# Clamping in VectorE's second pass, scaling of the weighed values on ScalarE or VectorE, and their addition to x on GpSimd

## The reference

```
x = x + 0.5 * ffn(layernorm(x)); x = x + attn(layernorm(x)); x = x + 0.5 * ffn(layernorm(x))

# attn, per head h and batch b, i >= j (causal)
s    = Re(qr_i . conj(kr_j))                       # q, k complex, 64 wide, rotated by position
E    = exp(clip(-mu * |i - j|, -30, 0))
V    = sigma_sq / (2 mu) * (1 - E*E) + eta_sq + gamma_sq
maha = maximum(qn_i + E*E * kn_j - 2 * E * s, 0) / V
logits = coef * log1p(maha / nu) - 0.5 * DH * log(V)
out  = softmax(logits) @ v;   y = [Re out, Im out] @ Wo
```

## Time and profile before

| | |
|---|---|
| median of 3 runs | 1684.14 us |
| profiled execution, its own time | 1685.38 us |
| its span, first to last instruction | 1683.6 us |
| matrix engine (PE), matmuls | 1624.1 us, 96% |
| VectorE (DVE) | 1494.5 us, 89% |
| ScalarE (ACT) | 1443.1 us, 86% |
| GpSimd (POOL) | 1013.6 us, 60% |

### The profile page before, as it was taken

The page is one execution under the profiler, slowest core; times in us unless marked ns, Lnnn a source line. Parts: engine busy times, 40 slices in busy tenths (PEclk is TensorE's granted clock), DMA queues, the critical chain, the costliest instruction groups (busy, mean ns, idle before and its releaser), DMA issues. The chain is left out here.

```text
span 1683.6 us, 31247 instructions
## 1 busy us (share of the span) xinstructions
PE 1624.1 (96%) x9690; PEld 1227.8 (73%) x9690; DVE 1494.5 (89%) x3380; ACT 1443.1 (86%) x2909; POOL 1013.6 (60%) x954
## 2 busy tenths in 40 slices
PE   5999988999999999999999999999999999899998
PEld 4787865777776777677777777777776776677876
DVE  6878878999999999999999999999999989977665
ACT  6677678999999999999999999999999998765765
POOL 3564556666666666665766666666666656245555
PEclk9999999999999999999999999999999999999999
DMA  6000022232223323232222323232232322100000
GB/s 178 1 1 1 1 97 73 64 92 64 76 70 76 79 64 85 58 82 70 75 74 64 92 64 76 55 92 69 74 84 60 80 59 51 26 8 7 13 13 13
DMA packets 50484, 100.05 MB, mean 59 GB/s; under 512 B 8208, under 2 KB 25872, under 8 KB 50320
## 3 DMA queue, kind: packets, MB, share of 16 engines
q1 hardware_dynamic: 50320, 98.07, 22.7%
HBM read 17.95 MB, written 5.24 MB: 14 GB/s over the span
## 5 line engine op out<-in xcount | busy, mean ns | idle before, releaser
L1500 POOL TENSOR_TENSOR early<-early 128x1024 f32<-128x1024 f32 x127 | 303.7, 2391 | 421.4 <-PE pS L1191 227.6
L661 POOL TENSOR_TENSOR hid_lo_d<-hid_d,hid_hi_d 128x512 fp32r<-128x512 f32 x176 | 231.4, 1315 | 218.4 <-ACT hid_hi_d L566 211.8
L1392 ACT ACTIVATE early<-early,qnorm 128x128 f32<-128x128 f32 (+3 forms) x512 | 246.6, 552 | 68.0 <-DVE early L1591 67.3
L1191 PE MATMUL pS<-early 128*128 128x128 f32 (+3 forms) x1024 | 297.6, 433 | 0.4 <-PEq L115 0.4
L1376 ACT ACTIVATE early<-early,nmax 128x128 f32<-128x128 f32 (+3 forms) x512 | 280.9, 558 | 7.7 <-DVE nmax L1578 7.4
L1191 PEld LDWEIGHTS pS<-early 128*128 128x128 f32 x1024 | 164.7, 191 | 96.1 <-issue 61.4
L1587 DVE SCALAR_TENSOR_TENSOR pS<-pS,ek 128x1280 f32<-128x1280 f32 x128 | 190.9, 1492 | 43.5 <-PE pS L1191 41.9
L1509 POOL TENSOR_TENSOR ek<-early 128x128 f32<-128x128 f32 (+3 forms) x256 | 216.1, 877 | 3.0 <-ACT early L1384 2.6
L1509 POOL TENSOR_TENSOR ek<-decay,early 128x128 f32<-128x128 f32 (+3 forms) x256 | 215.0, 873 | 0.0
L1233 PE MATMUL pS<-ident,early 128*128 128x128 f32 x1280 | 184.9, 278 | 13.3 <-DVE early L1591 7.0
L1405 ACT ACTIVATE early<-early,params 128x512 f32<-128x512 f32 (+1 forms) x256 | 196.4, 816 | 0.0
(11 more groups left out here) (393 smaller groups left out, 3752.5 us busy)
## 6 DMA issues: line engine op xcount, KB each, us to landing
early<-early SPq DMA_DIRECT2D x263, 256.0 KB, 3.4
early<-trig_d SPq DMA_DIRECT2D x64, 64.0 KB, 2.0
trig_d<-early SPq DMA_DIRECT2D x3, 1024.0 KB, 6.9
early<-in_w SPq DMA_DIRECT2D x3, 704.0 KB, 8.7
x_sb<-in_x SPq DMA_DIRECT2D x4, 512.0 KB, 8.3
early<-in_wqk SPq DMA_DIRECT2D x16, 128.0 KB, 3.4
cos<-trig_d SPq DMA_DIRECT2D x32, 64.0 KB, 2.2
sin<-trig_d SPq DMA_DIRECT2D x32, 64.0 KB, 2.0
```

The lines of the kernel that those rows point to most:

```text
L661: g.tensor_tensor(hid_lo[:, par], hid[:, par], hid_hi[:, par].bitcast(F32), ALU.subtract).then_inc(lo_done, 1)
L1191: last = pe.matmul(s.pS[:, span(I)], rot[:, I * P:(I + 1) * P], rot[:, N:N + (I + 1) * P], start=True, stop=True)
L1392: last = a.activation(u[:, span(I)], u[:, span(I)], ACT.Relu, bias=qnorm[:, r % 2, I:I + 1])
L1500: g.tensor_tensor(rot[:], by_cos[:], crossed[:], ALU.add).then_inc(S["rot_done"], 1)
```

## The change

- The clamp moves. GpSimd makes three columns for each pair from the query norms where it made one: `base` = query norm + U_MIN, `floor` = max(base * 2^-21, U_MIN), `low` = floor - base. The second pass on VectorE becomes four custom instructions (one per row tile) u = max(min(pS + ek, HIGHEST), low), and ScalarE's logarithm takes `base` as its bias, in four instructions where there were two. `clamp` is gone.
- The order of the product changes: the first pass multiplies, pS = -2 s * E, and the second adds ek, which is now E * E * kn. So ek is made from `decay2` and waits for it; it waits for the pair's second pass (t_done), where it waited for the first (w_done), because ek is now read there. `decay2` has two more buffers for even heads.
- `accumulate` is split. Scaling p7 by rinv into a new buffer `weighed` (512 columns, one buffer) is ScalarE's in steps of odd heads (four instructions, two ahead of soften and two behind key_norms) and VectorE's in the others (one instruction, ahead of `distances`). Adding `weighed` to x is GpSimd's, at the end of its step. The scaling waits for acc_done of the pair before; `weigh` waits for y_done (scaling) in place of acc_done.
- To make room in SBUF, the low half of W2 goes to DRAM at the start and comes back in step 123, both by a DMA from GpSimd.

The diff's core; the first `normalise_out` is ScalarE's, `accumulate` GpSimd's, the second `normalise_out` VectorE's.

```diff
             def distances(i, r):
-                wait(v, S["s_done"], n + 1)
-                wait(v, S["ek_done"], n + 1)
-                v.scalar_tensor_tensor(s.pS[:, 0:SW], s.pS[:, 0:SW], -2.0, ek[:], ALU.mult, ALU.add).then_inc(S["w_done"], 1)
-                wait(v, S["w_done"], n + 1)
+                v.wait_ge(S["decay_done"], i * 2 + r // B + 1)
+                wait(v, expanded[par], 48 * (i + 1) if par else 64 * i)
+                v.wait_ge(S["s_done"], n + 1)
+                v.scalar_tensor_tensor(s.pS[:, 0:SW], s.pS[:, 0:SW], -2.0, decay[par][:, 0:SW],
+                                       ALU.mult, ALU.mult).then_inc(S["w_done"], 1)
+                v.wait_ge(S["w_done"], n + 1)
+                v.wait_ge(S["ek_done"], n + 1)
+                v.wait_ge(S["qn_done"], n + 1)
                 wait(v, S["zred_done"], 2 * n)
-                for half, _ in HALVES:
-                    v.tensor_tensor(u[:, half], s.pS[:, half], decay[par][:, half], ALU.mult).then_inc(S["t_done"], 1)
+                for _, pieces in HALVES:
+                    for I in pieces:
+                        last = v._custom_dve(bass.dve_ops.TENSOR_ADD_SAT, out=u[:, span(I)], in0=s.pS[:, span(I)],
+                                             in1=ek[:, span(I)], s0=HIGHEST, s1=low[:, r % 2, I:I + 1])
+                    last.then_inc(S["t_done"], 1)
...
+            def on_scalar(i, r):
+
+                return (r + 3) % STEPS >= B and live(i, r + 3)
...
+            def normalise_out(i, r, tiles):
...
+                if 0 in tiles:
+                    a.wait_ge(S["av_done"], n + 1)
+                    a.wait_ge(S["rinv_done"], n + 1)
+                    wait(a, S["acc_done"], n)
+                for I in tiles:
+                    last = a.activation(weighed[:, I], s.p7[:, I * P:(I + 1) * P], ACT.Copy, scale=rinv[:, r % 4, I:I + 1])
...
+            def accumulate(i, r):
...
+                g.wait_ge(S["y_done"], n + 1)
+                xb = s.x_sb[:, b * TILES:(b + 1) * TILES, :]
+                g.tensor_tensor(xb, xb, weighed[:], ALU.add).then_inc(S["acc_done"], 1)
...
+            def normalise_out(i, r):
...
+                v.wait_ge(S["av_done"], n + 1)
+                v.wait_ge(S["rinv_done"], n + 1)
+                wait(v, S["acc_done"], n)
+                v.tensor_tensor(weighed[:], s.p7.rearrange("p (c d) -> p c d", c=TILES),
+                                rinv[:, r % 4, :].unsqueeze(2).broadcast_to([P, TILES, P]), ALU.mult).then_inc(S["y_done"], 1)
```

More of the change, by code:

```diff
@@ L1741, in a_step @@
                 if live(i, r):
[L1742 to L1743 removed]
+                    if live(i, r - 3) and not on_scalar(i, r - 3):
+                        normalise_out(i, r - 3)
                     distances(i, r)
@@ L1749, in a_step @@
                     query_norms(i, r + 1)
-                if live(i, r - 3) and n != PAIRS:
-                    accumulate(i, r - 3, range(TILES // 2 if live(i, r) else 0, TILES))
+                if live(i, r - 3) and n > PAIRS and not on_scalar(i, r - 3):
+                    normalise_out(i, r - 3)
                 if n == PAIRS:
```

125 lines of the change are left out of this document (73 added, 52 removed).

## The result

The changed kernel takes 1867.04 us (median of 4 runs, 1865.12 to 1867.17), the kernel before 1685.22 beside it (1682.43 to 1687.19): a ratio of 1.1078, 95% interval 1.1058 to 1.1097. That is 182 us more, where the prediction had 99. It lies outside the range, 19 us above its upper end.

A forecast was written before the change was run, and what follows sets the result against it. Even steps were bound by the matrix engine's chain through VectorE's second pass (9.86 us), odd ones by VectorE (8.85). Eight pairs of heads +84, last steps +15: 1685.4 + 99 - 1.2 = 1783 us, range 1728 to 1848.

The forecast's parts named there:

- The loop through acc_done: Within one step, from GpSimd's addition through ScalarE or VectorE and ek back: 9.36 us odd, 9.87 even, before contention.
- The first rival: GpSimd's added work stays hidden, the chain from addition through ScalarE and back under 8.6 us: 1679 or 1653 us, chance 6%.
- The fourth: Rival: the custom addition takes two cycles a column, making the second pass 1.33 us longer: about 1910 us, chance 3%.
- The third: Rival: VectorE's peaks run wholly in series with GpSimd: 1913 us at the extreme, 1848 half way, chance 10%.
- two operations of GpSimd delayed by 0.3 less a little give +0.4: Peaks meeting GpSimd's chain add 0.4 us a step, bounds 0 and 1.33: odd steps 9.75, even 10.27.
- the second pass, put at 1.75: VectorE's second pass as four custom instructions: 0.2 us more than its 1.55, straight into the even step's chain.
- the peaks' row (+0.5): Upper estimate for the second pass: a custom 384-column instruction takes 0.61 us against 0.46, so 0.5 for four.
- the pass's own rows (+0.18): Estimate for the second pass from 691 ns for 512 columns and 947 for 768: two more starts cost 0.18 us.
- The last steps: Last eight pairs: VectorE's moments wait for GpSimd's addition, three loops of 14.5 us: +18.6, net +15, bounds 8 and 28.
- The list: Signs: odd steps about 9.7 us, scaling waiting for GpSimd's addition, GpSimd over 80% busy, 384-column peaks 1 us in most steps.

The follow-up runs named there:

- e1: The changed kernel with two buffers for the weighed values, scaling waiting for the addition of two pairs before: 1752.61 us.
- e2: The changed kernel with GpSimd's addition moved ahead of ek in its step, still one buffer: 1729.93 us.
- e12: The changed kernel with one small GpSimd operation in place of three and a constant bound in the second pass: 1792.07 us.
- e6: The changed kernel with the last pairs' moments moved behind turn_parts and the reciprocal in VectorE's step: 1862.45 us.
- e3: The changed kernel with its new passes and small operations kept, but VectorE accumulating into x as before: 1741.81 us.
- e7: The changed kernel with the three small operations moved ahead of ek in GpSimd's step: 1988.74 us.
- e4: The kernel before with only scaling and addition split off, the clamp staying on ScalarE: 1737.38 us.
- e9: The kernel before without clamp or lower bound; in odd heads but the last, ScalarE scales and GpSimd adds after the peaks: 1669.03 us, ratio 0.9901.
- e8: e2 with the second pass as two plain additions, one small operation and no lower bound: 1696.8 us.
- e11: The kernel before, all computation kept; in odd heads but the last, VectorE scales in one instruction and GpSimd adds after the peaks: 1684.33 us, ratio 0.9991.

## Why the prediction was right and wrong

**Right: direction, place and mechanism.** The loop through acc_done runs as laid out, link by link, in both kinds of steps; the links that were mis-sized follow. e1 and e2 open it at two different points, and 114 and 137 of the 182 us go. The first rival (GpSimd's work hidden, 1679 or 1653 us) asked for a chain under 8.6; it is 10.17. The fourth (two cycles a column) is out: 1.93 us for 1280 columns. The third, the peaks in series with GpSimd, is where the truth lies in part: its half way was 1848, and the time is 19 above it. (Its 1.33 us for 1280 columns is a little much: the rows that the prediction reads give 1 ns a column, 1.28.)

**Wrong: the size of the contention, the step "two operations of GpSimd delayed by 0.3 less a little give +0.4".** I took one delay of 0.3, seen on one small operation in the earlier trace rows, and let it happen about twice, so 1.4 for the three small ones. They took 1.91 in the odd step, 1.80 in the even one, so the contention term, put at 0.4, was 0.9 and 0.8. The flaw is in what I took for the delay's size. It is not a property of the small operation but the rest of whatever peaks instruction it meets, in sequence: `base` asks at 1257.53, the 384-column peaks that have waited for ek run to 1257.95, the 512-column ones follow, and `base` ends after both. Its mean over all 128 pairs is 980 ns, that of `floor` 458, of `low` 244: 1.68 in all for 1.0. Groups of the changed kernel by line and shape:

```profile
L1546 POOL TENSOR_SCALAR base<-dist,params 128x4 f32<-128x4 f32 x128 | 125.4, 980 | 0.1
...
L1638 DVE CUSTOM_DVE_ANT_0 early<-pS,ek,low 128x384 f32<-128x384 f32 x128 | 77.8, 608 | 0.0
L1620 DVE CUSTOM_DVE_ANT_0 early<-early,lam,params 128x384 f32<-128x384 f32 x64 | 67.1, 1048 | 0.0
L1620 DVE CUSTOM_DVE_ANT_0 early<-early,lam,params 128x128 f32<-128x128 f32 x64 | 61.7, 964 | 0.1
```

**Wrong: the second pass, put at 1.75.** It takes 1.93. I weighed the peaks' row (+0.5) against the pass's own rows (+0.18) and took the latter; the per-partition operand, which neither row isolates, is worth 0.06 an instruction (0.24 for four, e12). In even steps this enters twice, on the path of the transposes and in front of ek: 0.18 of the miss.

**Wrong: nothing was put down for the even steps' other work.** The plain even step has 10.98 for 10.27 predicted: 0.4 more for contention of the small ones, 0.18 for the pass, 0.17 for ek (3.54, not 3.37). But three steps of an even head, in which VectorE builds tables, are 11.17 to 11.38, so the mean is 11.05. The building itself has become longer beside GpSimd's ek: the cast of 256 columns takes 0.53 to 0.55 us where it took 0.26 to 0.35, the multiplication of 512 columns by a column mostly 0.95 where it took 0.54.

**The account.** From the first pass of pair 0 to that of pair 127 were 1194.3 us before and are 1371.1 now. Of the +176.8, the last four steps (61.0 us, before 40.4) are +20.7, and the other 123 are +156.1 where the prediction had 84 less the 3.6 that it had in the odd steps of the end. By heads: an odd one of 82.2 us (8 x 10.28) for 78.0, an even one of 88.4 (8 x 11.05) for 82.2, so 10.4 us more than predicted for a pair of heads, and 76 us over the 123 steps. That is nearly all of the 83 us by which the change costs more than forecast. The last steps came out as predicted, +20.7 for +18.6 (gross), with 14.5 to 16.2 us for a step where 14.5 stood; that the peaks cost nothing extra there is luck of the phase, as e6 showed. In these steps the granted clock was 0.81 to 0.85 where it was 1.00 before, and 1.00 again in e2; the prediction had no term for it. It isn't seen on the path: VectorE's first passes there don't wait for the scores. Behind the last pair +3.8, not in my sum; e3, where VectorE accumulates, has +0.3 there and e2 +4.0, so it belongs to the split. The two transfers of W2's low half cost nothing that shows: the attention part starts at 260.0 us, before at 260.8.

**What would show it.** The list held but for two points: peaks of 384 columns are at 1.05 us in odd heads, but 0.65 to 0.71 in even ones, where the delay falls on those of 128 and 256 instead; and the odd steps were 10.2, not 9.7.

**Open.** Which of the two engines gets in first when both ask isn't settled by these runs. In the odd step the peaks of 384 and 512 columns go one after the other ahead of `base`, in e7 they go in turn with ek's pieces. e4's five steps say only that 0.03 us ahead was not enough for VectorE and 0.14 was. Which operands make a conflict rests on which instructions are stretched (the peaks, 0.61 to 2.72) and which are not (first pass, second pass and turn_parts, which read PSUM); no run gave the peaks an operand in PSUM. Two inputs in SBUF are not needed for it: the cast has one, of 256 columns, and takes 0.26 to 0.35 in the kernel before and in e9, 0.54 in the changed one, 0.71 in e3 and 0.9 in e8.

## What to carry to other kernels

A single buffer between two engines turns work that a share of 60% seems to have room for into a loop: before moving work to the idle engine, add up the chain from its last instruction through everyone who waits for it and back, and put the handed-over work at the front of that engine's step (137 of 182 us here).
When GpSimd and VectorE instructions with two SBUF inputs meet, price a meeting at the rest of the instruction that is met, and of the next one, not at a delay seen once; and look for what VectorE does next to a freed moment, since it may only reach the conflict earlier (e11).
VectorE's work with an operand in PSUM is the cover to place GpSimd's long instructions beside (e9).

## What the runs showed of the hardware

- GpSimd against VectorE with two SBUF operands is a lock of whole instructions and costs either side: the peaks' 384 columns alone 0.61 us, behind pieces of ek 1.07 and 1.61, behind a rotation 2.72; their 256 columns 0.48, 1.48 and 2.59; GpSimd's `base` 0.39 alone, 1.20 beside two of them. The Trainium skill, "SBUF — State Buffer", Who interferes with whom, says that the later of the two blocks for the whole instruction and that the order of issue decides who does; the 2.72 and 2.59 agree, and so does the rotation's 2.59 in e4, which started 0.14 us later. A small operation that is passed by two VectorE instructions in a row is more than that rule says, and in e4 an instruction of VectorE's with a start 0.03 us ahead of the rotation's was the one that waited.
- VectorE instructions with a single input in SBUF are stretched too: a 256-column cast 0.26 us in the kernel before, 0.54 in the changed one and 0.9 in e8, a 512-column multiplication by a column 0.54 and 0.95.
- Small GpSimd operations, each on the result of the one before, start 0.4 to 0.5 us apart though they have only 4 columns (976.90, 977.40, 977.80 in e7).
- Four custom additions that cover 1280 columns take 1.93 us with a per-partition bound and 1.69 with a constant; two plain ones without a bound take 1.55.
- A scaled 128-column copy out of PSUM on ScalarE takes 348 to 374 ns, two of them 0.62 together.
